# Second layer: two step-width products issued earlier, and identity products in three gaps of TensorE

## The chip, the cores and the metric

The kernel runs on one core of one Trainium2 chip. The core has five engines that run side by side, each with its own queue: TensorE (PE; its weight loads are listed as PEld), VectorE (DVE), ScalarE (ACT), GpSimd (POOL) and SyncE (SP, here the DMA queue). They wait for one another through semaphores. The metric is the device time of one execution in microseconds (us), as the median over runs.

## The reference

Two layers act on a residual x of 4 x 512 tokens of width 128. The first (a test-time-training layer and a small feed-forward) is not touched. The second normalises x to xn and adds two branches to it.

The state-space branch computes, for 256 channels:

```
u  = xn W_x^T + b_x ;  g = sigmoid(xn W_g^T + b_g)
u  = u * g + conv3(u) * (1 - g)
dt = clip(mean over tokens of softplus(xn W_dt^T + b_dt), 0.001, 2)
A  = -softplus(A_raw) ;  A_d = exp(A dt) ;  B_d = (A_d - 1) / (A + 1e-6) * B
state_t = A_d * state_(t-1) + B_d * u_t ;  y_t = sum_s state_t C
out = layernorm(xn + y W_out^T + b_out)
```

The expert branch takes a softmax over 8 gates, keeps the two largest, and computes for each of the 8 experts y = gelu(xn w1 + b1) w2 + b2; the two chosen experts' y are added, weighted by the sum of the two gates. All numbers are float32. x + both branches is the result.

## The kernel before, in words

The second layer stands in `layer1` (L1404). Every engine has a list of instructions written out by hand, in the order in which it runs them; there is no planner. `xn1T` holds the normalised tokens with features on the partitions. Work is cut into NU = 8 units n = (batch b, half of the channels k), each a product of 128 x 128 weights with 512 tokens into one PSUM bank; a float32 product shows as two matmul pieces in the trace.

**State-space inputs.** `u_product` (L1569, rows of L1573) fills banks 0 and 1, `gate_product` (L1575, L1579) banks 2 and 3, `dt_product` (L1581, L1585) banks 4 and 5. ScalarE empties them: `u_tile` (L1681: bias at L1686, first tap of the convolution at L1690), the sigmoid (L1710), and for dt an abs (L1723) and a relu with a running sum (L1726). Each product waits until ScalarE has emptied the bank two units back: `gate_done`, `u_done`, `relu_done`. After the eight units ScalarE takes exp and log of the abs (L1737, L1742), which completes the softplus; VectorE turns the sums into dt and A dt (L1883 to L1891). `conv` and `blend` on VectorE (L1833, L1843) make u; `gates` (L1792) makes the expert weights, which `turn_gates` (L1608, L1611) transposes on TensorE and `gate_rows` (L1820) copies.

**Experts.** Tokens go in four groups t of 512. `up(t, q)` (L1508, L1518) is the first product of expert pair q; `hidden` on ScalarE (L1674, L1679) applies the gelu into `he`; `picks(t, ...)` (L1520, L1531) spreads the gate rows over partitions with a product of two rows; `apply_gate` on VectorE (L1822, L1825) multiplies `he` by them and counts `gated`; `down(t)` (L1533, L1540 and L1542) is the second product, and `add_experts` (L1827, L1831) adds it to x and counts `y_done`. An up of unit n waits for `he_done` n - 1, picks of group t and down(t - 1) wait for `gated` 4t, and down(2) also waits for `y_done` 1, since it writes the bank that the first add reads.

**Scan.** The kernels of the chunked scan are made from A dt by ScalarE (`win` at L1755 after the hidden layers of group 2, d0 at L1763, the taps at L1695) and VectorE. `chunk_in` (L1545, L1550) and eight scans on VectorE (L1941) follow, then `chunk_out`, the output product and the last norm.

`keep_warm(nc, dst, square, n)` (L750, L753) issues n products of a 128 x 128 matrix with itself into a PSUM bank; nothing reads the result. It is used in the first layer already and at the start of the second.

The order of TensorE in the second layer stands from L1595 on, and it is what the diff edits:

Of the kernel before, what the change touches and what calls it, by code (L numbers as in the profile page):

```python
# [15 lines left out]
P = 128  # L16
# [733 lines left out]
def keep_warm(nc, dst, square, n):  # L750

    for _ in range(n):
        nc.tensor.matmul(dst, square, square, start=True, stop=True)  # L753
# [650 lines left out]
def layer1(nc, a, out, g):  # L1404
# [10 lines left out]
    sb, sem, con, bank, m1 = g["sb"], g["sem"], g["con"], g["bank"], g["m1"]  # L1415
# [4 lines left out]
    NU = 2 * B  # L1420
    with ExitStack() as c:
# [44 lines left out]
        up_mm, pick_mm, he_done, gated, down_mm, y_done = S("e_up", "e_pick", "he_done", "gated", "e_down", "y_done")  # L1466
        pads, u_mm, g_mm, dt_mm = S("pads", "u_mm", "g_mm", "dt_mm")
        u_done, gate_done, conv_done, diff_done, tap_done, uT_done = S(
            "u_done", "gate_done", "conv_done", "diff_done", "tap_done", "uT_done")
# [35 lines left out]
        with nc.Block() as block:  # L1505
            @block.tensor
            def _(pe):
                def up(t, q):  # L1508

                    n = 4 * t + q  # L1510
                    tok = slice(t * 512, t * 512 + 512)
                    if n >= 14:
                        pe.wait_ge(scanned, n - 9)
                    elif n >= 2:
                        pe.wait_ge(he_done, n - 1)
                    else:
                        pe.wait_ge(relu_done, NU - 1 + n)
                    nc.tensor.matmul(up_bank(n)[:, :], m1.w1[:, q, :], xn1T[:, tok], start=True, stop=True).then_inc(up_mm, 1)  # L1518

                def picks(t, qs):  # L1520

                    tok = slice(t * 512, t * 512 + 512)
                    pe.wait_ge(gT_done, 4)
                    pe.wait_ge(gate_done, NU)
                    if qs[0] == 2:
                        pe.wait_ge(scanned, 8)
                    elif t:
                        pe.wait_ge(gated, 4 * t)
                    for q in qs:
                        two = slice(32 * q, 32 * q + 2)  # L1530
                        nc.tensor.matmul(pick_bank(t, q)[:, :], con("pick")[two, :], gT[two, tok], start=True, stop=True).then_inc(pick_mm, 1)  # L1531

                def down(t):  # L1533
                    pe.wait_ge(gated, 4 * t + 4)

                    s, v = ((u_done, NU), (u_done, NU), (y_done, 1), (y_cp, 7))[t]
                    pe.wait_ge(s, v)
                    for i in range(4):
                        dst = down_banks[t][:, i * P:(i + 1) * P]
                        nc.tensor.matmul(dst, gT[:, t * 512 + i * P:t * 512 + (i + 1) * P], m1.b2[:], start=True, stop=False)  # L1540
                        for q in range(4):
                            mm = nc.tensor.matmul(dst, he[:, (4 * t + q) % 8, i * P:(i + 1) * P], m1.w2[:, q, :], start=False, stop=(q == 3))  # L1542
                    mm.then_inc(down_mm, 1)
# [25 lines left out]
                def u_product(n):  # L1569
                    b, k = divmod(n, 2)  # L1570
                    if n >= 2:
                        pe.wait_ge(u_done, n - 1)
                    nc.tensor.matmul(bank[n % 2][:, :], wT[:, 0, half(k)], xn1T[:, row(b)], start=True, stop=True).then_inc(u_mm, 1)  # L1573

                def gate_product(n):  # L1575
                    b, k = divmod(n, 2)
                    if n >= 2:
                        pe.wait_ge(gate_done, n - 1)
                    nc.tensor.matmul(bank[2 + n % 2][:, :], wT[:, 1, half(k)], xn1T[:, row(b)], start=True, stop=True).then_inc(g_mm, 1)  # L1579

                def dt_product(n):  # L1581
                    b, k = divmod(n, 2)
                    if n >= 2:
                        pe.wait_ge(relu_done, n - 1)
                    nc.tensor.matmul(bank[4 + n % 2][:, :], wT[:, 2, half(k)], xn1T[:, row(b)], start=True, stop=True).then_inc(dt_mm, 1)  # L1585
# [16 lines left out]
                gate_product(2)  # L1602
                gate_product(3)
                u_product(2)
                for n in range(4, NU):
                    gate_product(n)
                u_product(3)
                def turn_gates(i):  # L1608

                    for k in range(4):  # L1610
                        mm = nc.tensor.transpose(bank[6 + i % 2][:, k * P:(k + 1) * P],  # L1611
                                                 gt[:, 4 * i + k, :, :].rearrange("p q e -> p (q e)"), con("ident"))
                    mm.then_inc(gt_mm, 1)

                for n in range(NU):
                    dt_product(n)
                    if n == 1:
                        u_product(4)
                        pe.wait_ge(gates_done, 1)
                        turn_gates(0)  # L1620
                        turn_gates(1)
                    if n == 3:
                        pe.wait_ge(gT_done, 1)
                        turn_gates(2)
                        pe.wait_ge(gT_done, 2)
                        turn_gates(3)
                    if n == 5:
                        u_product(5)
# [7 lines left out]
                for t in (1, 2):  # L1636
                    up(t, 0)
                    up(t, 1)
                    picks(t, range(4))
                    down(t - 1)  # L1640
                    up(t, 2)
                    up(t, 3)
                down(2)
                pe.wait_ge(win_done, 8)
                pe.wait_ge(v_done, 2)
# [372 lines left out]
```

## Time and profile before

| | us |
|---|---|
| median of 3 runs (435.13, 437.49, 437.85) | 437.49 |
| the profiled execution's own time | 435.33 |
| its span, first to last instruction | 433.5 |
| mean granted TensorE clock | 0.947 of full speed |
| busy: PE 375.8, PEld 260.3, DVE 304.4, ACT 281.8, POOL 168.6 | of 433.5 |

Times in the trace count from the span's start. The second layer runs from about 294 us to the end. The time outside the span is what the execution takes before the first and after the last instruction.
### The profile page before, as it was taken

To read this page: it belongs to the slowest core of one execution; us is meant where nothing else is said; L and a number is where in the kernel's file an instruction comes from. 1 tells how busy PE (TensorE), PEld (TensorE's weight loads), DVE (VectorE), ACT (ScalarE), POOL (GpSimd) and SP (SyncE) were. 2 spreads that over 40 slices of the span, in tenths; PEclk is the share of its full clock that TensorE was granted. 3 is DMA by queue.
4 is the path that set the end of the run, shared out by engine and by line. 5 is a ranking of instruction groups with operands and counts; after the bars stand their busy time and mean duration, and the time that the engine had idled before them with its cause. 6 is when DMAs were issued, how large, how long until landed. Compare 5 with 4: busy or idle time off the path is not lost. (4 is left out here: it accounts for less than half of the span.)

```text
span 433.5 us, 10054 instructions
## 1 busy us (share of the span) xinstructions
PE 375.8 (87%) x3136; PEld 260.3 (60%) x3136; DVE 304.4 (70%) x1005; ACT 281.8 (65%) x691; POOL 168.6 (39%) x269
## 2 busy tenths in 40 slices
PE   1999999997999999999977999969788659688993
PEld 0454344366777777778764777766242435666982
DVE  4666809743998898889945578766989795374195
ACT  4687768473666666666627466646599942995634
POOL 1403919202788888888859032332000030000013
PEclk9999999998999999999999799989799688898997
DMA  8320323262122222222246100000000010000003
GB/s 230 60 81 9 107 73 106 60 176 79 45 76 76 73 73 73 73 73 63 65 153 148 23 1 2 0 2 0 1 2 1 0 27 2 1 2 0 2 0 98
DMA packets 33148, 23.14 MB, mean 53 GB/s; under 512 B 10062, under 2 KB 32860, under 8 KB 33116
## 3 DMA queue, kind: packets, MB, share of 16 engines
q1 hardware_dynamic: 31868, 22.67, 19.1%
q8 instruction: 16, 0.26, 0.3%
q10 hardware_dynamic: 1248, 0.07, 0.2%
q14 instruction: 16, 0.13, 0.1%
HBM read 13.26 MB, written 9.47 MB: 52 GB/s over the span
## 5 line engine op out<-in xcount | busy, mean ns | idle before, releaser
L486 PE MATMUL psum<-w,hT 128*128 128x385 f32 x128 | 45.5, 496 | 0.6 <-ACT stage L613 0.4
L900 PE MATMUL psum<-win,wst 128*32 128x128 f32 x1024 | 38.1, 279 | 1.3 <-ACT kd L975 1.3
L486 PEld LDWEIGHTS psum<-w,hT 128*128 128x128 f32 x128 | 23.2, 189 | 25.1 <-issue 11.4
L1004 ACT ACTIVATE std<-mv,cst 128x2 f32<-128x2 f32 (+1 forms) x34 | 10.0, 296 | 40.8 <-DVE mv L1142 38.4
L995 ACT ACTIVATE win<-psum 128x512 f32<-128x512 f32 x62 | 35.7, 581 | 0.0
L900 PEld LDWEIGHTS psum<-win,wst 128*32 128x32 f32 x1024 | 28.7, 110 | 5.6 <-ACT kd L975 1.5
L1272 ACT ACTIVATE std_<-mv_,cst 128x2 f32<-128x2 f32 (+1 forms) x46 | 13.5, 296 | 28.3 <-DVE mv_ L1250 16.4
L1500 POOL TENSOR_TENSOR win<-win,lng 128x512 f32<-128x512 f32 x2 | 2.5, 1272 | 71.2 <-ACT win L1785 71.2
L1057 POOL TENSOR_SCALAR xh<-raw,mv,rs 128x128 f32<-128x128 f32 x32 | 25.4, 795 | 3.2 <-DVE rs L1118 2.7
L1050 POOL TENSOR_TENSOR xkm<-win,wst 128x256 f32<-128x256 f32 x32 | 19.6, 614 | 15.3 <-PE psum L918 9.3
L1518 PE MATMUL psum<-xn1T,w1e 128*128 128x512 f32 x32 | 18.8, 714 | 7.7 <-ACT he L1679 6.1
L1222 POOL TENSOR_TENSOR xn<-xn,out_b 128x128 f32<-128x128 f32 x16 | 7.3, 454 | 42.6 <-ACT xn1T L1288 42.6
L1980 POOL MEMSET region<- 128x4096 f32 x1 | 3.5, 3512 | 50.6 <-ACT region L1742 50.6
L612 ACT ACTIVATE stage<-psum 128x384 f32<-128x384 f32 x32 | 15.7, 489 | 10.8 <-PE psum L486 9.4
L918 PE MATMUL psum<-grad,xkm 32*128 32x128 f32 x496 | 22.5, 296 | 0.0
L1045 POOL TENSOR_TENSOR cc<-win,wst 128x128 f32<-128x128 f32 x32 | 13.8, 432 | 21.6 <-POOLq L299 20.2
L1334 PE MATMUL psum<-region,tT 128*128 128x256 f32 x64 | 19.4, 429 | 0.0
L1542 PE MATMUL psum<-w2e,he 128*128 128x128 f32 x128 | 19.1, 298 | 0.0
L918 PEld LDWEIGHTS psum<-grad,xkm 32*128 32x128 f32 x496 | 16.6, 185 | 3.7
L910 PE MATMUL psum<-grad,masks 128*128 128x128 f32 x62 | 15.0, 324 | 3.9 <-DVE grad L1166 2.2
L1542 PEld LDWEIGHTS psum<-w2e,he 128*128 128x128 f32 x128 | 18.0, 217 | 0.0
L1679 ACT ACTIVATE he<-psum,b1e 128x512 f32<-128x512 f32 x16 | 10.5, 681 | 10.2 <-PE psum L1518 10.2
(307 smaller groups left out, 1142.4 us busy)
## 6 DMA issues: line engine op xcount, KB each, us to landing
rows_scratch<-stage SPq DMA_DIRECT2D x32, 192.5 KB
win<-rows_scratch SPq DMA_DIRECT2D x32, 192.5 KB, 2.4
attn_scratch<-ob SPq DMA_DIRECT2D x32, 64.0 KB
att<-attn_scratch SPq DMA_DIRECT2D x4, 512.0 KB, 4.0
xt<-in_L_attn_x SPq DMA_DIRECT2D x4, 256.0 KB, 4.2
out<-win SPq DMA_DIRECT2D x4, 256.0 KB, 2.4
cst<-in_constants SPq DMA_DIRECT2D x1, 408.0 KB, 5.1
w<-in_L_attn_wk SPq DMA_DIRECT2D x2, 128.0 KB, 4.2
```

Of the source, the lines that this page charges most:

```text
L486: mm = nc.tensor.matmul(rows_bank(i, h)[:, 0:RC], hT[:, k, i * P:(i + 1) * P], w4[:, k, h, :], start=(k == 0), stop=(k == 1))
L612: act.activation(stage[:, i % 2, h, 0:3 * F], src[:, 0:3 * F], ACT.Copy).then_inc(stage_done[h], 1)
L900: mm = nc.tensor.matmul(dst[32 * b:32 * b + 32, 0:F], v[:, at:at + 2 * K], w_sb[:, state, first_slot(b) + h, :], start=False, stop=(h == 1 ...
L910: nc.tensor.matmul(zbanks[(p + 1) % 2][:, 0:F], masks[:, (p + 1) % RING, P:2 * P], g_t, start=False, stop=True, skip_group_check=True).the ...
L918: mm = nc.tensor.matmul(bank[b][:, h * F:(h + 1) * F], xkm[own, p % 2, h, :], grad[own, p % 2, :], start=False, stop=False, skip_group_che ...
L995: nc.scalar.activation(own, psum[:, 2 * half:2 * half + 2, 0:H * F].rearrange("p b (h g) -> p b h g", h=H), ACT.Copy).then_inc(w_done, 1)
L1045: nc.gpsimd.tensor_tensor(cc[:, p % 2, :], rows[:, p, F:2 * F], ggb[:], ALU.add).then_inc(cc_done, 1)
L1050: nc.gpsimd.tensor_tensor(xkm[:, p % 2, :, :], rows[:, p, 0:F][:, None, :].broadcast_to([P, H, F]), headt[:, :, None].broadcast_to([P, H, ...
L1057: nc.gpsimd.tensor_scalar(xh[:], raw[:, p, :], mv2[:, p % 2, 0, 0:1], rs2[:, p % 2, 0:1], ALU.subtract, ALU.mult).then_inc(xg_done, 1)
L1334: ins = nc.tensor.matmul(dst, tT[:, 1 - p, 0, k * P:(k + 1) * P], wo[:, k, :], start=False, stop=(k == 1))
L1518: nc.tensor.matmul(up_bank(n)[:, :], m1.w1[:, q, :], xn1T[:, tok], start=True, stop=True).then_inc(up_mm, 1)
L1542: mm = nc.tensor.matmul(dst, he[:, (4 * t + q) % 8, i * P:(i + 1) * P], m1.w2[:, q, :], start=False, stop=(q == 3))
```

## The change

Two edits, both in TensorE's list in `layer1`. First, `dt_product(0)` and `dt_product(1)` are issued ahead of `gate_product(4)` rather than after `u_product(3)`; the loop over the other dt products keeps its order, and what stood between dt products 1 and 2 (`u_product(4)`, the turning of the first gates) is now right behind `u_product(3)`. Second, three calls of `keep_warm` with the identity matrix: eight products between up(1, 1) and picks(1), behind a wait for all eight u_tiles (they write bank 1, which u products used); sixteen between down(0) and up(1, 2), into the same bank; six ahead of down(2), into bank 0, behind a wait for `y_done` 1. The other engines' lists and the DMAs are as before.

```
                 gate_product(3)
                 u_product(2)
+                dt_product(0)
+                dt_product(1)
                 for n in range(4, NU):
                     gate_product(n)
                 u_product(3)
...
-                for n in range(NU):
-                    dt_product(n)
-                    if n == 1:
+                for n in range(1, NU):
+                    if n > 1:
+                        dt_product(n)
+                    else:
                         u_product(4)
                         pe.wait_ge(gates_done, 1)
                         turn_gates(0)
...
                 for t in (1, 2):
                     up(t, 0)
                     up(t, 1)
+                    if t == 1:
+                        pe.wait_ge(u_done, NU)
+                        keep_warm(nc, bank[1][:, 0:P], con("ident"), 8)
                     picks(t, range(4))
                     down(t - 1)
+                    if t == 1:
+                        keep_warm(nc, bank[1][:, 0:P], con("ident"), 16)
                     up(t, 2)
                     up(t, 3)
+                pe.wait_ge(y_done, 1)
+                keep_warm(nc, bank[0][:, 0:P], con("ident"), 6)
                 down(2)
```

## Rows read from the trace of the kernel before

**Rows 1.** Chain of waits, 290 to 380 us: start us, us, engine, tile, line.

```profile
315.10 1.72 PE psum L1585 x4
...
354.47 6.69 PE psum L1518 x8
361.16 1.07 PE psum L1531 x8
```

**Rows 2.** Stretches; busy us (count) PE, PEld, DVE, ACT, POOL; granted clock, DMA share, GB/s.

```profile
309.40:312.70 3.30, 3.30 (x5) 1.30 (x4) 3.16 (x32) 2.40 (x4) 0.00 (x0) 0.50 0.00 0
312.80:340.00 27.20, 21.71 (x66) 9.06 (x64) 24.52 (x37) 25.85 (x44) 0.00 (x0) 1.00 0.00 1
340.10:346.80 6.70, 5.49 (x24) 4.02 (x25) 4.68 (x4) 6.67 (x7) 0.00 (x0) 0.50 0.00 0
...
353.70:360.50 6.80, 6.03 (x7) 2.43 (x8) 6.63 (x13) 3.16 (x6) 0.00 (x0) 0.50 0.15 35
360.60:370.70 10.10, 8.01 (x54) 5.46 (x52) 5.07 (x10) 3.48 (x6) 0.00 (x0) 1.00 0.01 2
370.80:374.10 3.30, 2.85 (x13) 2.85 (x14) 0.40 (x1) 3.25 (x5) 0.00 (x0) 0.50 0.00 0
...
394.70:398.00 3.30, 3.30 (x15) 2.85 (x14) 0.64 (x2) 0.00 (x0) 0.00 (x0) 0.50 0.00 0
```

**Rows 3.** Timeline, ScalarE, sigmoids to third abs; brackets: idle before, releaser.

```profile
310.70 0.67 ACT L1710 ACTIVATE region<-psum,bg 128x512 f32<-128x512 f32 x1
312.23 0.69 ACT L1710 ACTIVATE region<-psum,bg 128x512 f32<-128x512 f32 x1 [0.86 <-PE psum L1579]
313.42 0.69 ACT L1710 ACTIVATE region<-psum,bg 128x512 f32<-128x512 f32 x1 [0.50 <-PE psum L1579]
314.28 0.69 ACT L1710 ACTIVATE region<-psum,bg 128x512 f32<-128x512 f32 x1 [0.17 <-PE psum L1579]
315.14 0.69 ACT L1686 ACTIVATE region<-psum,bx 128x512 f32<-128x512 f32 x1 [0.17 <-PE psum L1573]
...
319.44 0.69 ACT L1723 ACTIVATE region<-psum,bd 128x512 f32<-128x512 f32 x1 [0.28 <-PE psum L1585]
```

**Rows 4.** Timeline, TensorE, the pauses named in the prediction.

```profile
308.84 5.40 PE L1579 MATMUL psum<-xn1T,wT 128*128 128x512 f32 x8 [2.82 <-ACT region L1710]
...
323.53 1.13 PE L1585 MATMUL psum<-xn1T,wT 128*128 128x512 f32 x2 [1.46 <-ACT he L1726]
...
341.31 2.09 PE L1531 MATMUL psum<-ffnT,cst 2*128 2x512 f32 x8 [3.30 <-DVE he L1825]
...
348.68 1.06 PE L1542 MATMUL psum<-w2e,he 128*128 128x128 f32 x8
354.47 6.69 PE L1518 MATMUL psum<-xn1T,w1e 128*128 128x512 f32 x8 [4.74 <-ACT he L1679]
...
371.25 0.80 PE L1540 MATMUL psum<-b2e,ffnT 128*128 128x128 f32 x2 [2.64 <-DVE he L1825]
...
393.87 1.35 PE L1531 MATMUL psum<-ffnT,cst 2*128 2x512 f32 x4 [1.48 <-DVE uT L1944]
```

**Rows 5.** Timeline, VectorE, from the turned gates to the first scan.

```profile
318.15 1.29 DVE L1820 COPY ffnT<-psum 128x512 f32<-128x512 f32 x2 [1.85 <-PE psum L1611]
...
360.19 0.69 DVE L1825 TENSOR_TENSOR he<-he,psum 128x512 f32<-128x512 f32 x1
...
366.93 0.69 DVE L1831 TENSOR_TENSOR xt<-xt,psum 128x512 f32<-128x512 f32 x1 [3.89 <-PE psum L1542]
...
381.18 1.22 DVE L1941 TENSOR_TENSOR_SCAN uT<-d,psum 128x512 f32<-128x512 f32 x1 [2.49 <-PE psum L1550]
```

**Rows 6.** Timeline, ScalarE, group 2's hidden layer and d0.

```profile
367.79 0.69 ACT L1679 ACTIVATE he<-psum,b1e 128x512 f32<-128x512 f32 x1 [5.91 <-PE psum L1518]
...
377.58 3.51 ACT L1763 ACTIVATE d<-a 128x3968 f32<-128x3968 f32 x1
```

**Rows 7.** Timeline, TensorE, sixteen identity products in the first layer.

```profile
221.42 3.84 PE L753 MATMUL psum<-cst 128*128 128x128 f32 x32
```

More of the change, by code:

```diff
@@ L1604, in _ @@
                 u_product(2)
+                dt_product(0)
+                dt_product(1)
                 for n in range(4, NU):
@@ L1613, in turn_gates @@
                     mm.then_inc(gt_mm, 1)
-                for n in range(NU):
-                    dt_product(n)
-                    if n == 1:
+                for n in range(1, NU):
+                    if n > 1:
+                        dt_product(n)
+                    else:
                         u_product(4)
@@ L1638, in _ @@
                     up(t, 1)
+                    if t == 1:
+                        pe.wait_ge(u_done, NU)
+                        keep_warm(nc, bank[1][:, 0:P], con("ident"), 8)
                     picks(t, range(4))
                     down(t - 1)
+                    if t == 1:
+                        keep_warm(nc, bank[1][:, 0:P], con("ident"), 16)
                     up(t, 2)
                     up(t, 3)
+                pe.wait_ge(y_done, 1)
+                keep_warm(nc, bank[0][:, 0:P], con("ident"), 6)
                 down(2)
```

## Prediction

> **What bounds the kernel now.** The profiled execution took 435.33 us, of which the span is 433.5; the other 1.83 us lie outside the trace and I leave them alone. Both edits lie between 300 and 380 us, so I read the chain of waits there first. It runs through TensorE's gate products, then ScalarE's chain of abs, relu and hidden layers, then a few small VectorE steps, then eight pieces of up at 354.47 (6.69 us), the picks at 361.16 and down(1) [rows 1]. The reader should see that no engine is the bound throughout: the end is set in turn by TensorE, ScalarE and VectorE, each waiting for another.
>
> Then I read the granted clock by stretch [rows 2]. It is 0.50 (1.2 GHz) from 309.40 to 312.70, 340.10 to 346.80, 353.70 to 360.50, 370.80 to 374.10 and 394.70 to 398.00, and 1.00 (2.4 GHz) in the two stretches between that stand beside them. Last come TensorE's pauses [rows 4]: the clock fell during or just after pauses of 2.82, 3.30, 4.74 (the one ahead of 354.47), 2.64 and 1.48 us, and held through one of 1.46 us. The question for each slow stretch is who waits for it.
>
> **The change, part by part.**
>
> *The two step-width products moved ahead of the gate products.* Nothing is added; four pieces of matmul move earlier. They need only xn1T and banks 4 and 5, which are free. Two products take 1.72 us at the full clock [rows 1], and they fall into the 2.82 us pause [rows 4] in which TensorE waits for ScalarE's sigmoids. At half clock they would take 3.44 us and hold gate_product(4) back 0.6 us; its sigmoid starts at 310.70 [rows 3], behind other ScalarE work, so the product (308.84 plus 0.86 is 309.70) has 1.0 us to spare. The move itself costs nothing.
>
> It should give this. With the pause reduced to 1.1 us I expect the full clock to hold through the gate products. ScalarE's pauses there were 0.86 and 0.50 before two sigmoids, and 0.17 before the last sigmoid and before u_tile(3), which began at 315.14 [rows 3]. At 0.86 us a product: product 4 ends 309.70, product 5 310.56, product 6 waits for the sigmoid that ends 311.37 and ends 312.23, product 7 ends 313.09, u_product(3) 313.95, and u_tile(3) begins about 313.99. That is 1.15 us earlier. The third abs then finds its step-width product ready, since TensorE has no dt products 0 and 1 and no queue behind u_product(3): its 0.28 us pause goes [rows 3]. ScalarE is 1.43 us earlier. VectorE must follow: its 1.85 us pause for the turned gates [rows 5] goes as well, since u_product(4) and the turning come forward by more than 1.4 us. Its slack is thus larger than ScalarE's gain, and the 1.43 us pass through to the logs on ScalarE, the small step-size instructions on VectorE, GpSimd's memset (released by the same logs, so it moves along) and so to the gating ahead of the picks.
>
> Bounds for this part: if the clock stays low here all the same, only the 0.28 remain; if all five pauses vanish, 1.98. I take 1.43 because it follows the order of waits.
>
> The Trainium skill speaks against this part (TensorE: Matmul & The Clock Gate, section "A second HAM failure mode: psum-queue depth-cycling"): short pauses between groups that cycle through PSUM banks make the clock swing, and the re-warming is paid again and again. By that rule the gate products, which alternate between two banks and still pause, would stay slow. The trace does not bear it out: from 312.80 to 340.00 TensorE pauses often, once for 1.46 us, and the clock stays at 1.00 [rows 2, 4].
>
> *Eight identity products between up(1,1) and picks(1).* Sixteen of them took 3.84 us at the full clock [rows 7], so eight take 1.9, at most 3.8 at half. The pause is 3.30 us [rows 4], and picks(1) start when VectorE has gated the first four. The new wait for the eighth u_tile holds nothing: up(1,1) already waits for a hidden layer that ScalarE issues after it. What this could speed up is picks(1) and down(0), 341.31 to 349.74 at half clock [rows 4]. But nobody waits there: the next ups wait for ScalarE until 354.47. Gain nought; if the products ran slow, 0.5 us late, hidden by the same 4.74 us.
>
> *Sixteen after down(0).* 3.84 us at full, at most 7.7 at half, into 4.74 us. So they cost between nought and 3.0 us; I take nought, since down(0)'s last eight pieces (1.06 us at 348.68 [rows 4]) show that the clock is up again by its end. What could be won is the up stage: 6.69 us of eight pieces against 3.44 at 0.86 a product [rows 1]. But picks(2) also wait for VectorE's eighth gating, which ends at 360.88 (360.19 plus 0.69) [rows 5], while the ups end at 361.16. So at most 0.28 us can be won. I count all of it.
>
> *Six ahead of down(2).* 1.4 us into a pause of 2.64 [rows 4]. The wait for y_done is met, because VectorE's add_experts(0) stands ahead of the gating at 360.19 on its queue. Down(2) now runs partly at half clock [rows 2], and it may end over 1 us earlier. That pays nothing: VectorE's first scan begins at 381.18 [rows 5], when ScalarE's d0 is ready (377.58 plus 3.51 is 381.09), and ScalarE works from 367.79 [rows 6] to there with hardly a pause. Its start depends on down(1)'s end, through up(2,2). The trace puts the scan's wait down to the chunk products; d0's end, 0.09 us ahead of the scan, is the likelier releaser, and if it is not, what is won here is at most the slow stretch of down(2), some 1.5 us.
>
> No DMA is moved, and SP's and GpSimd's queues keep their order.
>
> **Sum.** 1.43 + 0.28 = 1.71 us. The profiled execution would go from 435.33 to 433.6. It lies 2.16 us below the median of the three runs, 437.49; from that I get 435.8, the forecast.
>
> **The rivals.**
>
> *The slow clock moves into down(1): slower.* The half-clock ups are hidden today; they happen to fill the time until VectorE's eighth gating. If the identity products keep TensorE fast, the ups end near 356.5 (354.47 less 1.43, plus 3.44) and the picks can't start before 359.4 (360.88 less 1.43). That is a new pause of 2.9 us, the size after which the clock fell before [rows 4], and the next work is picks(2) and down(1), which are on the path. They took 5.77 us at the full clock (361.16 to 366.93) [rows 1, 5]; the same instructions for the first group took 8.43 at half [rows 4], 2.66 more. Result: 435.8 + 2.7 = 438.5. At the very worst the 5.77 double: 441.6. It decides as soon as the fall costs more than 1.71. For it: the pause. Against it: it needs the sixteen products to end close to 353.0. If down(0) runs at the full clock it is done in 5.8 us instead of 8.4, the sixteen end near 349.5 (339.9 + 5.8 + 3.8), and a pause of 3.5 us remains, after which the ups are slow as now and nothing is lost. So it hangs on whether the clock falls in what is left of the 3.30 us pause, about 1.4 us: 1.46 held and 1.48 fell [rows 4].
>
> *The gate stretch does not gain.* The clock may stay low there by the rule cited, or it may not have been low in the usual execution. Then only 0.28 + 0.28 are won: 436.9. For it: the shown runs differ by 2.7 us, so executions do differ in such stretches. Against it: the 2.82 us pause is in every execution, and in this one the clock fell after every pause of that size.
>
> **How the numbers follow.** Forecast 0.52, slow down(1) 0.26, no gain at the gates 0.22. The forecast's own range is 433.6 (profiled execution less the sum) to 436.5. With the rivals, 433.5 to 438.3 leaves out the upper half of the first rival (0.13) and some 0.05 at the other ends. One per cent, about what a measurement of this kernel can tell from no change, is 4.4 us; the best sum of bounds is 1.98 + 0.28, so faster than 433.1 needs the low end of the runs as well: 0.09. Slower than 441.9 needs all of down(1) and more at half clock: 0.03. Within: 0.88.
>
> **What would show it.** Right: granted clock 1.00 from 309 to 313; no ScalarE pause over 0.3 us before the sigmoids; no VectorE pause before the first turned gates; ln_done about 1.4 us earlier; picks(2) begin as the eighth gating ends; scan 0 still begins as ScalarE's d0 ends. The first rival: ups done near 356.5, clock 0.50 in down(1), and hidden(2,2) not earlier than 367.79. The second: clock 0.50 among gate products 5 to 7. The forecast is wrong if the whole moves by more than 2.3 us either way, or if down(2)'s end proves to set the scan.

## The result and the profile after

The changed kernel took 433.96 us, the median of 20 runs (431.37 to 437.37); the kernel before, timed with it, 435.28 (428.88 to 438.58, 20 runs). The ratio of the two is 1.0062, with a 95% interval of 1.0032 to 1.0091: slower by 0.6 per cent, where 0.4 per cent faster was forecast. This ratio, like all ratios below, leaves out executions more than 1.5% above a kernel's fastest: half of the runs of the kernel before, which alone has executions of 429, and none of the changed kernel's. The text therefore goes by means over all runs: 434.48 and 434.27 over 20 each (standard deviations 2.85 and 1.83, so 0.2 with an uncertainty of 0.75, which is one standard error, here and below). What has to be explained is thus not a loss of 0.6 per cent but a change that moves the mean by nothing that can be told, and has neither the best executions nor the worst.

The profiled execution of the changed kernel took 431.75 us, span 430.0. First the granted clock by stretch (columns as in [rows 2]):

```profile
306.60:309.90 3.30, 3.30 (x5) 1.00 (x4) 3.16 (x24) 2.10 (x4) 0.00 (x0) 0.50 0.00 0
309.90:350.90 41.00, 31.26 (x157) 18.54 (x155) 36.48 (x52) 36.64 (x55) 3.51 (x1) 1.00 0.01 3
351.00:354.30 3.30, 3.30 (x4) 1.37 (x5) 3.16 (x8) 1.12 (x2) 0.00 (x0) 0.50 0.32 52
354.40:391.80 37.40, 30.36 (x193) 21.77 (x192) 22.63 (x39) 28.27 (x28) 0.00 (x0) 1.00 0.00 1
391.90:395.20 3.30, 3.30 (x18) 3.30 (x17) 0.00 (x0) 0.55 (x1) 0.00 (x0) 0.50 0.00 0
```

Two of the slow stretches of [rows 2] are gone, 340.10 to 346.80 and 370.80 to 374.10. But the gate products have theirs still (306.60 to 309.90), and chunk_out too (391.90 to 395.20). TensorE's timeline shows why the first remained. These lines answer to [rows 4]:

```profile
299.97 1.02 PE L1573 MATMUL psum<-xn1T,wT 128*128 128x512 f32 x2
300.83 1.88 PE L1585 MATMUL psum<-xn1T,wT 128*128 128x512 f32 x4
305.52 5.46 PE L1579 MATMUL psum<-xn1T,wT 128*128 128x512 f32 x8 [2.81 <-ACT region L1720]
...
337.75 1.14 PE L1531 MATMUL psum<-ffnT,cst 2*128 2x512 f32 x8 [1.52 <-DVE he L1835]
...
343.39 3.74 PE L753 MATMUL psum<-cst 128*128 128x128 f32 x32
350.91 5.57 PE L1518 MATMUL psum<-xn1T,w1e 128*128 128x512 f32 x8 [3.79 <-ACT he L1689]
357.46 1.14 PE L1531 MATMUL psum<-ffnT,cst 2*128 2x512 f32 x8 [0.98 <-DVE he L1835]
...
367.62 0.49 PE L1540 MATMUL psum<-b2e,ffnT 128*128 128x128 f32 x2 [1.30 <-DVE he L1835]
```

The pause ahead of the gate products is 2.81 us, as long as before, although the dt products (L1585) now stand in it. In this execution the u and gate products before them had run at the full clock; without the dt products the pause would have been some 4.5. In the execution of before they had run at half clock up to 306.0 and had filled those 1.7 us themselves. These are the slow stretch, which the prediction's list leaves out, and u_product(2) in it, both of the kernel before:

```profile
302.60:305.90 3.30, 3.30 (x5) 0.82 (x3) 3.16 (x6) 0.00 (x0) 0.00 (x0) 0.50 0.00 0
304.11 1.91 PE L1573 MATMUL psum<-xn1T,wT 128*128 128x512 f32 x2
```

ScalarE's lines that answer to [rows 3]:

```profile
308.37 0.69 ACT L1720 ACTIVATE region<-psum,bg 128x512 f32<-128x512 f32 x1 [0.33 <-PE psum L1579]
310.16 0.69 ACT L1720 ACTIVATE region<-psum,bg 128x512 f32<-128x512 f32 x1 [1.11 <-PE psum L1579]
311.02 0.69 ACT L1720 ACTIVATE region<-psum,bg 128x512 f32<-128x512 f32 x1 [0.17 <-PE psum L1579]
311.88 0.69 ACT L1696 ACTIVATE region<-psum,bx 128x512 f32<-128x512 f32 x1 [0.17 <-PE psum L1573]
...
315.88 0.69 ACT L1733 ACTIVATE region<-psum,bd 128x512 f32<-128x512 f32 x1
```

The pauses add up to 1.78, against 1.70 before; only the 0.28 before the third abs is gone. VectorE's lines, for [rows 5], and ScalarE's d0, for [rows 6]:

```profile
313.17 1.29 DVE L1830 COPY ffnT<-psum 128x512 f32<-128x512 f32 x2 [0.20 <-PE psum L1613]
...
377.55 1.22 DVE L1951 TENSOR_TENSOR_SCAN uT<-d,psum 128x512 f32<-128x512 f32 x1 [3.02 <-ACT d L1773]
373.95 3.51 ACT L1773 ACTIVATE d<-a 128x3968 f32<-128x3968 f32 x1
```

The 1.85 us before the turned gates are down to 0.20. The first scan's wait is now put down to ScalarE's d0, which ends 0.09 us ahead of it (373.95 plus 3.51 is 377.46).

The second layer, from its first u product (291.17) to the end, took 138.83 us; before it took 138.99 (294.51 to 433.5). So nearly all of the 3.5 us between the two spans lie in the first layer, whose code is the same.

### The profile page after: what moved, and what is told of

Its sections match the earlier page's. It is cut to its first block and busy times, and to the rows that moved or that the text cites. A ratio compares the mean times of both kernels' runs of the same rounds, so it can differ in the third digit from the quotient of the medians.

```text
span 430.0 us, 10174 instructions
## 1 busy us (share of the span) xinstructions
PE 372.5 (87%) x3196; PEld 260.7 (61%) x3196; DVE 304.9 (71%) x1005; ACT 281.8 (66%) x691; POOL 168.8 (39%) x269
## 5 line engine op out<-in xcount | busy, mean ns | idle before, releaser
L1518 PE MATMUL psum<-xn1T,w1e 128*128 128x512 f32 x32 | 17.7, 672 | 6.7 <-ACT he L1689 5.1
L1045 POOL TENSOR_TENSOR cc<-win,wst 128x128 f32<-128x128 f32 x32 | 13.9, 433 | 21.6 <-POOLq L299 20.2
L753 PEld LDWEIGHTS psum<-cst 128*128 128x128 f32 x152 | 19.3, 204 | 3.2 <-issue 3.0
L753 PE MATMUL psum<-cst 128*128 128x128 f32 x152 | 19.8, 288 | 1.7 <-PEq L824 1.7
L1334 PE MATMUL psum<-region,tT 128*128 128x256 f32 x64 | 18.1, 405 | 0.0
```

The source lines that it names most:

```text
L1334: ins = nc.tensor.matmul(dst, tT[:, 1 - p, 0, k * P:(k + 1) * P], wo[:, k, :], start=False, stop=(k == 1))
```

## The experiments

The theories. **Theory 1:** the moments at which the clock may change are not tied to the program; each execution meets them elsewhere, and a time is the sum of the slow stretches on which something waits. The dt products gain, and something takes it back. **Rivals:** the change costs in every execution; or the identity products move a slow stretch into down(1), the first rival of the prediction.

The readings of all profiles stand in one table, so that each verdict below can point at a row. Column 1 is the start of the first u product, in us from the span's start; the others count from there: the end of ScalarE's logs (read at the start of the read-out of the last one's sum, 1.8 us after that log began, and called "last log" below), the start of VectorE's second add_experts (when down(1) is done), the time from the first chunk_out piece to the first transpose of y, and the length of the second layer (span less column 1).

| profile | first layer's end | last log | down(1) done | chunk_out to y | second layer |
|---|---|---|---|---|---|
| before | 294.51 | 52.11 | 72.42 | 17.05 | 138.99 |
| e1 before again | 293.28 | 52.10 | 72.42 | 17.07 | 139.02 |
| e5 before, 0.9 later | 293.10 | 52.09 | 72.31 | 15.68 | 137.30 |
| e6 before, 1.8 later | 294.55 | 51.21 | 71.45 | 18.08 | 139.75 |
| e13 before, first layer filled | 291.30 | 52.14 | 72.36 | 18.55 | 140.60 |
| after | 291.17 | 51.89 | 72.13 | 17.31 | 138.83 |
| e2 change again | 293.50 | 50.95 | 71.19 | 17.31 | 137.80 |
| e7 change, 0.9 later | 294.80 | 50.91 | 71.16 | 17.31 | 137.80 |
| e8 change, 1.8 later | 298.63 | 50.92 | 72.80 | 17.31 | 139.47 |
| e14 change, first layer filled | 290.86 | 50.95 | 71.18 | 17.31 | 137.84 |
| e3 dt only | 297.04 | 50.98 | 71.22 | 17.31 | 137.86 |
| e17 dt only, first layer filled | 291.11 | 50.95 | 71.19 | 17.31 | 137.79 |
| e4 identity only | 289.81 | 53.45 | 73.69 | 17.31 | 140.39 |
| e15 identity only, first layer filled | 291.07 | 51.27 | 73.13 | 17.31 | 139.73 |
| e9 scans filled | 291.27 | 53.50 | 73.74 | 15.68 | 138.73 |
| e10 dt, gates filled | 295.70 | 50.99 | 71.24 | 17.31 | 137.90 |
| e11 dt, gates and scans filled | 296.86 | 50.96 | 72.81 | 15.68 | 137.84 |
| e12 change, gates and scans filled | 297.10 | 50.99 | 71.23 | 15.68 | 136.30 |
| e16 the same, first layer filled | 290.43 | 50.96 | 71.19 | 15.68 | 136.17 |
| e18 e11, first layer filled | 290.85 | 50.94 | 71.19 | 15.68 | 136.15 |

**e1 and e2: both kernels again, without an edit.**

> The kernel before, unchanged, timed and profiled once more. Theory 1 (the moments at which TensorE's clock falls are not tied to the program, and the spread of a kernel's times is how many of those stretches lie where something waits for TensorE): the times spread over 8 us or more again, the mean within 1 us of the kernel before beside it, and this profile's clock falls at other places than in the first profile; the time from the start of u_product(0) to the first gate_product after the pause stays 14.3 us, but the pause in front of it grows by about 1.7 us (to 4.5) if the u products ran at the full clock. Theory 2 (the spread is noise of another kind): the clock falls at the same places, and the times do not follow the mean granted clock.

> The changed kernel, unchanged, timed and profiled once more. Theory 1: mean within 1 us of the kernel before beside it, spread about 6 us, and no execution as fast as the best of the kernel before (429); times fall by about 1 us for each slow stretch less. Theory 2 (the change makes every execution 0.6 per cent slower): the mean is 2.6 us above that of the kernel before.

Measured with 29 runs of the kernel before beside them (mean 433.95): e1 428.64 to 438.05, mean 432.78 of 12, which is 1.2 under with an uncertainty of 1.2; e2 431.76 to 437.4, mean 433.78 of 12. Theory 1 holds for the spread: the time follows the mean granted clock. The five fastest executions of e1 (428.6 to 430.1) have a clock of 0.975 or 0.976, its three slowest (437.5 to 438.1) 0.936 to 0.948. It is wrong on one point: e1's clock fell in the second layer at the same places as in the first profile, within 0.1 us counted from the first u product, so not every execution differs. Theory 2 for e2, 2.6 us more, is out.

e2's profile shows what the dt products do when u products run slow ahead of them. TensorE:

```profile
303.14 1.87 PE L1573 MATMUL psum<-xn1T,wT 128*128 128x512 f32 x2
304.85 1.88 PE L1585 MATMUL psum<-xn1T,wT 128*128 128x512 f32 x4
307.84 1.98 PE L1579 MATMUL psum<-xn1T,wT 128*128 128x512 f32 x4 [1.11 <-ACT region L1720]
310.41 1.98 PE L1579 MATMUL psum<-xn1T,wT 128*128 128x512 f32 x4 [0.59 <-ACT region L1720]
```

and its granted clock over that stretch:

```profile
301.50:304.80 3.30, 3.30 (x5) 1.27 (x4) 3.16 (x6) 0.03 (x1) 0.00 (x0) 0.50 0.00 0
304.90:352.60 47.70, 36.27 (x168) 20.52 (x167) 43.33 (x111) 42.45 (x64) 3.51 (x1) 1.00 0.01 3
```

This is the case that the prediction worked out: a pause of 1.11, no slow gate product after it, and the last log 1.15 us earlier than in both profiles of the kernel before.

**e3 and e4: each part alone.** e3 leaves out the three `keep_warm` calls; e4 leaves the dt products where they were.

```
 e3:  -  pe.wait_ge(u_done, NU); keep_warm(..., 8)
      -  keep_warm(..., 16)
      -  pe.wait_ge(y_done, 1); keep_warm(..., 6)
 e4:  -  dt_product(0); dt_product(1)   ahead of gate_product(4)
```

> The earlier dt products alone, no identity products. By the forecast's first term this gives 1.4 us where the clock was low among the gate products, and 0.3 us elsewhere: mean 0.5 to 1.4 us under the kernel before. Rival (the identity products carry the loss, by a slow clock in picks(2) and down(1)): this kernel is faster than the full change by 1 us or more. Other rival (the moved dt products cost): it is as slow as or slower than the kernel before.

> The identity products alone, the dt products where they were. By the forecast nought to 0.3 us won in the mean. Rival (they move the slow clock into picks(2) and down(1)): 1 to 2.7 us slower than the kernel before, with the ups of the pause done near 357, a pause of over 2 us behind them, and a granted clock of 0.50 in down(1).

e3: mean 434.28 of 12 (ratio 0.9996, 0.9947 to 1.0045). That is 0.3 over the kernel before and 0.5 over e2, each with an uncertainty of 1.0, so the gain expected of e3 isn't seen. e4: mean 436.52 of 7 (ratio 1.0103, 1.0031 to 1.0175). So the forecast for e4, nought to 0.3 won, is not borne out: this kernel was slower. What cost it isn't shown. Its profile is of the fastest of the seven executions (431.95) and doesn't show the rival at work; the loss in it lies among the gate products (last log at 53.45), which stand ahead of all identity products. With 7 to 12 runs of such a spread these means can't carry more.

**e5 to e8: the second layer shifted.** Four or eight identity products ahead of `u_product(0)`, in the kernel before (e5, e6) and in the change (e7, e8).

```
+                keep_warm(nc, bank[7][:, 0:P], con("ident"), 4)    # 8 in e6, e8
                 u_product(0)
```

> The kernel before with four identity products ahead of u_product(0): the second layer starts some 0.9 us later against the moments at which the clock may change. Theory 1 (what the second layer takes depends on where these moments fall): measured from the first u product, the layer's length is not 139.0 as in both profiles of the kernel before but shorter or longer by 1 us or more, through the gate products (ScalarE's pauses at its sigmoids) or through the first chunk_out. Theory 2 (the length is a property of the program): 139.0 again, 0.2 either way.

> The same with eight products, some 1.8 us later. Theory 1: another length again, and somewhere in this scan one near 137, which the kernel before needs for its best executions (429): there the clock falls neither among the gate products nor in chunk_out. Theory 2: 139.0.

> The changed kernel with four identity products ahead of u_product(0). Theory 1: its length differs from 137.8 and 138.8 of its two profiles; the dt products hold the clock where they come behind slow u products (pause 1.1 us), and not where the u products ran fast (pause 2.8 us). Rival (the identity products before the picks lose the best case): where the ups run at the full clock, a pause of over 2 us stands ahead of picks(2) and down(1) is slow.

> The same with eight products. Theory 1: another length, and where neither the gate products nor chunk_out are slow, 136.3 or less. Rival: no length under 137.5 in either of the two shifted kernels, because down(1) or chunk_out is slow in every case.

The lengths are 137.30 and 139.75 for the kernel before, 137.80 and 139.47 for the change: theory 1, against the 139.0 of theory 2. Two of its readings missed: e7 has the length of e2's profile, where another was expected, and e8's rival came true, no length under 137.5 in e7 and e8, with chunk_out slow in both. (The totals hold the added products as well: means of 434.95, 437.02, 436.20 and 439.35 beside 434.46. The change is 1.3 and 2.3 over the kernel before shifted alike, with uncertainties of 1.7 and 1.5.) In e5 the gate products are slow as ever, but nothing is slow from 358.40 to 426.50, when TensorE's last product has ended:

```profile
351.60:358.30 6.70, 5.27 (x6) 2.09 (x7) 6.56 (x12) 3.32 (x5) 0.00 (x0) 0.50 0.18 40
358.40:426.50 68.10, 57.01 (x415) 46.92 (x413) 36.79 (x85) 45.19 (x58) 5.08 (x4) 1.00 0.02 5
```

Chunk_out then takes 15.68 rather than the 17.05 of before, and those 1.4 us come off the end. That is the kind of execution in which the kernel before is at its best; whether its 429 us are this case isn't shown, since none of them was profiled. Whether chunk_out meets a slow stretch isn't set by its place in the program: it began 100.32 us after the first u product in e5 and 100.30 in e6, where it was slow and took 18.08:

```profile
393.10:399.90 6.80, 6.80 (x27) 5.29 (x27) 1.26 (x2) 1.55 (x2) 0.00 (x0) 0.50 0.00 0
```

e8 shows the rival. TensorE from the identity products on, and the clock:

```profile
351.50 3.74 PE L753 MATMUL psum<-cst 128*128 128x128 f32 x32
357.40 3.89 PE L1518 MATMUL psum<-xn1T,w1e 128*128 128x512 f32 x8 [2.17 <-ACT he L1690]
363.96 1.14 PE L1531 MATMUL psum<-ffnT,cst 2*128 2x512 f32 x8 [2.68 <-DVE he L1836]
```

```profile
345.90:349.20 3.30, 3.30 (x17) 3.30 (x17) 1.83 (x2) 3.30 (x4) 0.00 (x0) 0.50 0.00 0
349.30:366.30 17.00, 12.16 (x80) 8.62 (x80) 14.63 (x26) 7.88 (x12) 3.51 (x1) 1.00 0.08 18
366.40:369.70 3.30, 3.30 (x18) 3.30 (x17) 0.00 (x0) 0.00 (x0) 0.00 (x0) 0.50 0.00 0
```

The clock fell at 345.85, just behind picks(1), which follow the 1.51 us that the eight products had left of the pause ahead of them. Down(0) was slow for 3.3 us, the sixteen ended late, so the ups came fast (3.89 rather than 5.4 to 6.7 us), TensorE then paused 2.68 us for VectorE, and the clock fell inside down(1). It was done 21.88 us after the last log (72.80 less 50.92), against 20.24 in e2: 1.64 us, in the length and on the path. The pause ahead of picks(1) is 1.51 or 1.52 us in all nine profiles with the three groups; the clock held behind it in seven and fell in two, e8 and e15, so its length alone doesn't decide.

**e9 to e12: filling the places that are on the path.** e9, in the kernel before, fills the pauses among the scans; e10, on e3's kernel, the rest of the pause ahead of the gate products; e11 has both; e12 is the full change with both.

```
 e9:  +  pe.wait_ge(scanned, 5); keep_warm(nc, bank[0][:, 0:P], con("ident"), 3)
         up(3, 2)
      +  pe.wait_ge(scanned, 6); keep_warm(nc, bank[1][:, 0:P], con("ident"), 2)
         up(3, 3)
      +  pe.wait_ge(scanned, 7); keep_warm(nc, bank[2][:, 0:P], con("ident"), 3)
         picks(3, (2, 3))
 e10:    dt_product(1)
      +  keep_warm(nc, bank[6][:, 0:P], con("ident"), 6)
```

> The kernel before with identity products among the scans: three ahead of up(3, 2), two ahead of up(3, 3), three ahead of picks(3, (2, 3)), each behind the scan that frees the bank it writes, and nothing else. Theory 1 (the slow stretch in chunk_out, which the gain at the gates only shifts, is on the path and costs 1.4 us): the first chunk_out to the first transpose of y takes 15.7 us rather than 17.1 to 17.3, the second layer about 137.6, and the mean of the times falls by 0.8 to 1.4 us. Rival (something else sets the end there, the result copies on ScalarE, say): 15.7 us is not reached or the length stays 139.

> The earlier dt products without the three groups of identity products, and six identity products right behind them in the same pause (bank 6). Theory 1 (the dt products hold the clock only behind slow u products, since the pause is 2.8 us behind fast ones): the clock never falls among the gate products, u_tile(3) begins 19.8 us after the first u product whatever came before, the logs end at 50.95. Alone it may win little in the mean, for chunk_out then meets its slow stretch in most executions: mean within 1 us of the kernel before. Rival (the forecast as it stood: the gain passes through): mean 1.4 us faster.

> Both of these: earlier dt products with six identity products behind them, the identity products among the scans, and none ahead of or behind down(0) and down(1). Theory 1: the second layer takes 136.2 to 136.5 us, every execution gains, and the mean is 2 us or more under the kernel before. Rival (gains do not add, a third place takes them back): 137.5 or more.

> The full change with both fillings. Theory 1 (the three groups of identity products bring nothing to the end, and now and then move a slow stretch into down(1), which costs 1.6): not faster than the kernel without the three groups, 0 to 0.6 us slower in the mean. Rival (they are of use once the rest is repaired): 0.3 us faster or more.

Beside 35 runs of the kernel before (mean 434.87), the means of 12 are 433.79, 434.51, 433.63 and 434.13 (ratios 1.0041, 0.9999 to 1.0083; 1.0004, 0.9949 to 1.0059; 0.997, 0.9906 to 1.0034; 1.0041, 0.9998 to 1.0084). The means lie 0.4 to 1.2 under, with uncertainties of 0.6 to 1.0, and can't tell the kernels apart. The lengths settle the stages: chunk_out takes 15.68 in every profile with filled scans, the last log stands at 50.96 to 50.99 with filled gates, and e12's layer takes 136.30, 2.7 less than before. The gains in the totals are smaller than that. In the profiles the first layer ended at 295.7 to 297.1 in three of the four, which would hide them; whether it did so in the other executions isn't shown. Against what was expected: e9's layer is 138.73 rather than 137.6, for its gate products were slower (last log at 53.50); e10 is as theory 1 has it; e12's mean is 0.5 over e11's, inside theory 1's range, but with an uncertainty of 0.9. e11's length, 137.84, is the rival's, and contradicts me: it has none of the three identity groups, and yet a slow stretch in down(1) (72.81). That stretch is thus not theirs alone:

```profile
363.30:366.60 3.30, 3.30 (x19) 3.30 (x16) 0.69 (x1) 0.00 (x0) 0.00 (x0) 0.50 0.00 0
```

**e13 to e18: the same on an even first layer.** Identity products in pauses of the first layer, alike in all six: four more at the end of its input stage, five before its first scan step, four in some turns of its output stage.

```
 input stage:   keep_warm(..., 10)  ->  keep_warm(..., 14)
 scan stage:    + keep_warm(nc, bank[3][:, 0:P], con("ident"), 5)      ahead of the first wait
 output stage:  + elif n > NT + 1: keep_warm(nc, bank[2 if n < NT + 4 else 3][:, 0:P], con("ident"), 4)
                + elif n in (1, 3): keep_warm(nc, bank[6][:, 0:P], con("ident"), 4)
```

> The kernel before with identity products in pauses of TensorE in the first layer alone (four more at the end of its input stage, five ahead of the first scan step, four in four or five turns of its output stage). Theory 1 (most of the spread is the clock in the first layer): its end lies at 290 to 292 us rather than 290 to 297, the spread shrinks to 4 us or less, and the mean falls by 2 us or more. Theory 2 (the spread comes from elsewhere): the times spread as before.

> The whole change on top of the first layer's filling. Theory 1 (the gain at the gates is real but chunk_out's slow stretch takes it back in part): 0 to 1.3 us under the kernel with the filling alone. The forecast as it stood: 1.7 us under it. Rival (the change costs): over it.

> The three groups of identity products on top of the first layer's filling, without the earlier dt products. Theory 1 (they end where nobody waits): within 0.6 us of the kernel with the filling alone. Rival (they cost of themselves, as e4's mean suggests): 1.5 us or more over it.

> The change with the six products behind the dt products, the eight among the scans, and the first layer's filling. Theory 1: second layer 136.3 us in most executions, first layer's end at 290 to 292, so a mean of 428 to 430: 4 us or more under the kernel before. Rival (gains in one place are taken back in another): 432 or more.

> The earlier dt products alone on the first layer's filling. If the change is a gain and a loss added (identity groups +1.5 by the means of e13 and e15): 1.1 us under the filling alone, near 430.6, logs at 50.95 after the first u product. If the dt products win nothing in the mean and the groups' cost is an accident of the sample: 431.7 or more.

> All fillings and the earlier dt products, without the three groups of identity products. If the groups only cost (a slow stretch in down(1) when they keep the ups fast): under e16's 431.1 (nine executions without the one of 479). If the slow stretch in down(1) comes without them as well, as in e11's profile: equal or slower, 431 to 432.5.

The first layer's end lay between 290.43 and 291.30 in all six profiles, and the standard deviations are 0.4 to 1.7 (e16 without its execution of 479.11), against 2.7 for the kernel before beside e13 to e16 and 1.9 beside e17 and e18 (without its 875.58). The first layer's filling alone took the mean from 434.67 to 431.71; its times still spread over 4.8 us, where 4 or less was expected. Means of 12 executions, first layer filled:

| us | dt products as before | dt products earlier |
|---|---|---|
| no identity groups | 431.71 (e13) | 430.56 (e17) |
| identity groups | 433.24 (e15) | 432.10 (e14) |

The earlier dt products win 1.15 and 1.14, the identity groups lose 1.53 and 1.54. Averaged over both columns or rows, each effect has a standard error of 0.4 (from the spreads of 0.8 to 1.7); their sum, the whole change, is 0.4 slower with an error of 0.6. e17 was timed in another session and on another chip than the other three; taken against the kernel before beside each, it is 0.8 under e13 rather than 1.15. So, with the first layer filled, the change is a gain and a somewhat larger loss that cancel within the error. e14 thus came out over e13, where theory 1 and the forecast had it under, e15's rival held, and e17 is where the sum of gain and loss had put it. The groups raise the mean granted clock (0.976 in e15's executions against 0.971 in e13's) and lose time all the same.

The profiles support the gain. Without the early dt products the last log stands at 51.2 to 53.5, on the mean of eight profiles 52.2; with them and without the gate filling it stands at 51.1 on the mean of seven. They do not account for the whole loss: from the last log to the end of down(1) it is 21.9 us rather than 20.2 to 20.3 in two of the nine profiles with the groups and in one of the eleven without (e11), which makes 0.2 us on the mean and not 1.5.

e15's profile is e8's case once more:

```profile
344.30 3.74 PE L753 MATMUL psum<-cst 128*128 128x128 f32 x32
350.18 3.89 PE L1523 MATMUL psum<-xn1T,w1e 128*128 128x512 f32 x8 [2.15 <-ACT he L1691]
356.73 1.14 PE L1536 MATMUL psum<-ffnT,cst 2*128 2x512 f32 x8 [2.66 <-DVE he L1837]
```

```profile
338.30:341.60 3.30, 3.30 (x16) 3.30 (x17) 2.23 (x2) 3.29 (x5) 0.00 (x0) 0.50 0.00 0
...
358.70:362.00 3.30, 3.30 (x18) 3.30 (x17) 0.00 (x0) 0.00 (x0) 0.00 (x0) 0.50 0.00 0
```

**The version that beats both** is e18: the earlier dt products, all the fillings, and none of the three groups. Six executions took 428.04 to 428.99, median 428.51, against 434.52 for the kernel before beside it: ratio 0.9862, interval 0.9816 to 0.9909. e16, the same with the three groups, has a median of 431.82 in 10 executions (ratio 0.9914, 0.9875 to 0.9952), of which nine average 431.08, short of the 428 to 430 that theory 1 expected, and one took 479.11 at a mean clock of 0.754. That one stays unexplained, as does one of 875.58 of the kernel before. e18 lies 2.6 us under those nine, as the loss by the groups would have it, though it too was timed on another chip. In e18 the clock still falls where nobody waits:

```profile
336.60:343.30 6.70, 6.70 (x30) 5.20 (x31) 4.57 (x6) 6.63 (x8) 1.26 (x1) 0.50 0.01 2
343.40:350.20 6.80, 2.70 (x21) 2.24 (x20) 6.61 (x10) 3.41 (x5) 2.15 (x1) 1.00 0.12 22
350.30:353.50 3.20, 3.20 (x5) 1.16 (x4) 3.06 (x9) 1.25 (x2) 0.00 (x0) 0.50 0.32 44
353.70:367.10 13.40, 9.61 (x62) 6.58 (x61) 7.60 (x14) 5.37 (x7) 0.00 (x0) 1.00 0.00 1
367.30:370.50 3.20, 3.20 (x17) 3.20 (x17) 0.00 (x0) 3.15 (x5) 0.00 (x0) 0.50 0.02 5
370.70:421.80 51.10, 47.06 (x354) 40.54 (x353) 29.35 (x73) 35.47 (x45) 5.07 (x4) 1.00 0.02 6
```

Slow down(0), slow ups, slow down(2), and a second layer of 136.15, the shortest of all. The reader should see that a clock of 0.974 here beats one of 0.984 in e14's profile (span 427.0 against 428.7).

## Why the prediction failed

The forecast was 435.8 and faster; the median came at 433.96, and the comparison gave no gain. That 433.96 lies inside the stated range is luck: the kernel before, too, came 2.2 us lower over 20 runs (435.28) than over the three that the forecast was counted from (437.49). By its own steps:

- **What waits for whom: right.** Slow down(0) and slow down(2) cost nothing; with down(2) 1.4 us shorter, the first scan still began as d0 ended, 0.09 us behind it after, in e2 and in e18 as in [rows 5, 6]. In all twenty profiles the first scan begins 14.25 or 14.26 us after the second add_experts, whenever down(2) ended, and e17 and e14, with these stages slow and fast, have layers of 137.79 and 137.84.
- **The dt products: right in mechanism, too big, and not always there.** The move costs nothing (the gate product after the pause begins 14.35 us after the first u product, 14.33 before). The gain is 1.15, not 1.43: the 0.28 before the third abs goes, but u_tile(3) begins 0.84 and not 1.15 earlier (19.79 after the first u product in e2, 20.63 before), since one sigmoid still pauses 0.64 in e2, where I had allowed 0.3. It is 1.15 against the two profiles of the kernel before; against e6 and e15, where the gate products ran fast without the early dt products, it is 0.3. In the profile of the changed kernel it fell to 0.2, for a reason that the prediction missed: it took the 2.82 us pause as a property of the program, while its length depends on whether the products before it ran fast. Its list of slow stretches leaves out the one at 302.6 to 305.9, in which u_product(2) ran. The rival "the gate stretch does not gain" named the outcome, with another cause. The rule cited with it, that short pauses between groups which cycle through PSUM banks make the clock swing (the Trainium skill, TensorE: Matmul & The Clock Gate, section "A second HAM failure mode: psum-queue depth-cycling"), isn't borne out by e2: gate products in two banks with pauses of 1.11 and 0.59, clock 1.00 throughout.
- **"So at most 0.28 us can be won. I count all of it": wrong.** From the last log to picks(2) it is 14.47 us before and 14.40 in e2, so 0.07, and e3 has the same 14.40 without any identity product, so even the 0.07 isn't theirs.
- **"I take nought" for the sixteen products: this is the step that failed.** With the first layer filled the three groups cost 1.5 us in the mean, with an error of 0.4. Without the filling the means are mixed: 2.6 slower in e4 against the kernel before, 0.5 faster in e2 against e3, 0.5 slower in e12 against e11, each with an error of about 1. The one mechanism of a cost that the profiles show is the first rival, to the letter in e8 and e15, and it costs 1.64 where it happens, against the 2.66 of the forecast. I had given it 0.26. No run leaves out one group of the three, so the share of the sixteen isn't measured by itself. I argued that a pause of 3.5 us would stay ahead of the ups, which held in seven of the nine profiles with the groups (3.78 to 3.80; the other two are e8 and e15), and weighed the fall in down(0) as a toss-up. Whether down(1) alone makes up the mean loss stays open. e14's executions fall into five with a clock near 0.984, as the profiled one, and seven near 0.975 that are 2.1 us longer on the mean. That is two more stretches of 3.3 us at half clock (2 x 3.3 x 0.5 of 430 us is 0.008), but where they lie isn't known, since none of the seven was profiled.
- **The sum against the median: wrong in kind.** I took one profiled execution 2.2 us under the median and carried a difference over. The first layer's end alone lay between 289.8 and 298.6 us in the profiles, 7 us of difference in code that is the same (1.8 of it e8's added products).

What took the gain back was thus, by the means with the first layer filled, the identity groups. That it was the same in the kernels without that filling is argued from there and not shown: e3, which has no groups, gained nothing that could be told. Chunk_out's 1.4 us is on the path, as e5, e9 and e12 show. It doesn't take the gain back in the profiles: it is slow in before and in e2, 17.05 and 17.31, and 1.19 us still come off the length. e13 and e17 can't be compared for it, since chunk_out takes 18.55 in one and 17.31 in the other.

## What to carry to other kernels

Ask of every slow stretch of TensorE who waits for its work before filling the pause ahead of it: here moving the dt products, filling the pauses ahead of such work and leaving three others slow gave 6 us, 3 of them in the first layer, while filling the other three lost 1.5. A stage that runs slow but still ends in time also keeps TensorE busy up to the next wait; make it fast and the pause moves behind it, as in e8 and e15. And where executions of one program differ by more than the effect sought, even out the unrelated part first and compare the parts of the change in all four combinations.

## What was not expected of the hardware

Executions of one program on one core spread over 10 us (428.6 to 438.7 for the kernel before), and the time goes with the mean granted clock, 0.976 to 0.936. The places at which the clock changes differ between executions of the same code: in the first layer it fell at 100.5 us in e12 and not at all in e4. Twice in all runs an execution was far off: 479.11 with a clock of 0.754, and 875.58 with a clock given as 1.00.
